# One VectorE filler calendar replaced by a fixed pattern, and gi laid out with the whole block as its last axis: a GRU and mixture-of-experts kernel

## What is computed

```python
def cell(h, x):                       # 512 times, B = 4, D = 512
    gi = x @ W_ih + b_ih              # r, z, n
    gh = h @ W_hh + b_hh
    r = sigmoid(i_r + h_r); z = sigmoid(i_z + h_z)
    n = tanh(i_n + r * h_n)
    return (1 - z) * n + z * h
...
x = x + moe_lora(scan(cell, cond_2048, x))          # layer 0
...
ix = (grid + 1) * 0.5 * (L - 1); x0 = floor(ix)     # layer 1
cond = w0 * x[x0] + w1 * x[x0 + 1]                  # along the features
x = x + experts_top2(cond)
```

## Time and profile before

| | |
|---|---|
| median of 3 runs | 2057.33 us (2053.76 to 2059.42) |
| the profiled execution | 2053.76 us, its span 2051.9 us |
| TensorE matmul busy | 1696.2 us, 83% |
| TensorE weight load busy | 1095.2 us, 53% |
| VectorE busy | 1410.8 us, 69% |
| ScalarE busy | 750.2 us, 37% |
| GpSimd busy | 285.6 us, 14% |
| mean granted TensorE clock | 0.966 |

### The profile page before, as it was taken

How to read it: one execution, slowest core, us unless ns; L and a number is a source line. 1 busy time by engine, 2 the same in 40 slices (tenths; PEclk the granted TensorE clock), 3 DMA queues, 4 the chain that set the end, 5 groups by cost and what they waited for, 6 DMA issues and landing times. The chain is left out here.

```text
span 2051.9 us, 90285 instructions
## 1 busy us (share of the span) xinstructions
PE 1696.2 (83%) x38301; PEld 1095.2 (53%) x38301; DVE 1410.8 (69%) x6376; ACT 750.2 (37%) x2706; POOL 285.6 (14%) x581
## 2 busy tenths in 40 slices
PE   6777767778679999968599999978699999776995
PEld 4565555555445556545456566545456555442442
DVE  6888888887757777767677777767677777641221
ACT  5544444442323343322233343323233333322332
POOL 0111111121121111120211011120211111201001
PEclk9999999999989999999899999989899999987997
DMA  8444343422055464422265555240545464228995
GB/s 311 174 145 157 129 157 141 157 95 85 22 204 193 172 248 176 144 64 64 85 213 185 210 214 178 82 116 3 186 183 193 172 213 152 69 60 304 348 356 164
DMA packets 113621, 334.86 MB, mean 163 GB/s; under 512 B 41920, under 2 KB 42168, under 8 KB 100800
## 3 DMA queue, kind: packets, MB, share of 16 engines
q1 hardware_dynamic: 108096, 312.31, 42.8%
q0 software_dynamic: 5120, 16.78, 2.5%
HBM read 263.74 MB, written 65.32 MB: 160 GB/s over the span
## 5 line engine op out<-in xcount | busy, mean ns | idle before, releaser
L480 PE MATMUL bank_g<-whh,hs_early 128*32 128x256 f16 x8192 | 324.6, 279 | 257.7 <-DVE hs_early L972 247.9
L1261 POOL COPY hxs<-hs 128x32 f16<-128x32 f16 x512 | 221.7, 433 | 1519.6 <-DVE hs L977 1519.6
L727 ACT ACTIVATE rz<-pre 128x32 f32<-128x32 f32 x512 | 118.9, 232 | 804.2 <-DVE pre L960 804.2
L480 PEld LDWEIGHTS bank_g<-whh,hs_early 128*32 128x32 f16 x8192 | 173.8, 97 | 435.0 <-DVE hs_early L972 424.0
L958 DVE STREAM_TRANSPOSE xt<-bank_g 128x256 f32<-128x256 f32 x512 | 229.7, 449 | 201.8 <-PE bank_g L486 196.4
L626 PE MATMUL bank<-wm,wih 128*128 128x512 f16 x1440 | 351.1, 384 | 2.8 <-issue 1.6
L493 PE MATMUL bank_g<-whh,hs 128*32 128x128 f16 x16384 | 331.4, 222 | 6.6 <-issue 6.1
L486 PE MATMUL bank_g<-whh,hs 128*32 128x256 f16 x8192 | 321.6, 278 | 1.4 <-issue 1.1
L493 PEld LDWEIGHTS bank_g<-whh,hs 128*32 128x32 f16 x16384 | 290.5, 99 | 14.0 <-issue 10.3
L727 ACT ACTIVATE seq_h<-na 128x16 f32<-128x16 f32 x512 | 111.6, 218 | 283.2 <-DVE na L966 283.2
L486 PEld LDWEIGHTS bank_g<-whh,hs 128*32 128x32 f16 x8192 | 191.1, 98 | 43.5 <-DVE hs L977 3.3
(11 more groups left out here) (139 smaller groups left out, 1863.4 us busy)
## 6 DMA issues: line engine op xcount, KB each, us to landing
wm<-moe_split SPq DMA_DIRECT2D x60, 1536.0 KB
wm<-moe_split SPq DMA_DIRECT2D x60, 1024.0 KB
wm<-moe_split SPq DMA_DIRECT2D x60, 512.0 KB
wm<-in_w_moe SPq DMA_DIRECT2D x16, 1536.0 KB, 10.9
moe_split<-wm SPq DMA_DIRECT2D x16, 1536.0 KB, 6.4
wih<-x_rows SPq DMA_DIRECT2D x60, 256.0 KB, 7.6
y_rows<-wih SPq DMA_DIRECT2D x60, 256.0 KB, 4.9
xr<-in_x SPq DMA_DIRECT2D x16, 512.0 KB, 7.0
```

Source lines behind the costliest of these rows:

```text
L480: mm(bank_g[0][32 * j:32 * j + 32, 0:2 * P], early_cols[:, 4 * B * k:4 * B * k + 32], whh[:, 1, k, at:at + 2 * P], start=(k == 0), stop=False)
L727: return nc.scalar.activation(dst, src, func, **kw)
L1261: Q.tensor_copy(hxs[:, par, :, :, :, col].rearrange("p s k b -> p s (k b)"), hs_new).then_inc(S["h_kept"], 1)
```

## The change

Two edits. First, the order of the fillers: GRID_AT is replaced by one pattern of steps for each sequence (GRID_STEPS, relative to step 32 b), whatever else stands in those steps; the layer-0 parts go to the VectorE steps 20 q + 10 and + 11, their ScalarE copy into step 20 q + 10 itself, and SyncE asks for the next grid row and the next layer-0 part at other steps. Second, gi is laid out as [128, 12, 4, 128]: the two halves lie side by side in each row of 128 time steps, so a half is 48 runs of 64 values. No arithmetic changes.

```diff
-def grid_steps():
-    at, s = {}, -1
-    for b in range(B):
-        s = max(s, 32 * b - 1)
-        for j in range(GRID_CHAIN):
-            s += 1 if j < 4 or j % 3 != 1 else 2
-            while s in X_LO or s in L0_LO or s == 97:
-                s += 1
-            at[s] = (b, j)
-    return at
+GRID_STEPS = (0, 2) + tuple(4 + 7 * k + o for k in range(K) for o in (0, 1, 4))
...
-        gi = sb("gi", [P, 2, G3, B, TB], F32)
+        gi = sb("gi", [P, G3, B, FT], F32)
...
+        def grid_at(s):
+            return s // 32, GRID_STEPS.index(s % 32) if s % 32 in GRID_STEPS else None
...
# sync: gi_half
-                sp.dma_start(gates_in[VISITS[v]]...[:, m], gi[:, at, m]
-                             ).then_inc(gi_stored[q], 16)
+                sp.dma_start(gates_in[VISITS[v]]...[:, m],
+                             gi[:, m, :, at:at + TB]).then_inc(gi_stored[q], 16)
...
-                if s % 32 == 5 and s // 32 + 1 < B:
+                if s % 32 == 3 and s // 32 + 1 < B:
...
-                if s - 3 in L0_AT[:3]:
-                    load_l0(L0_AT.index(s - 3) + 1)
+                if s % 20 == 15 and s // 20 < 3:
+                    load_l0(s // 20 + 1)
...
# sync: gi_load
-                sp.dma_start(gi[:, half].rearrange("p m b t -> p (m b t)"), gates_in[q]).then_inc(gi_in[half], 16)
+                sp.dma_start(gi[:, :, :, half * TB:(half + 1) * TB],
+                             gates_in[q].rearrange("p (m b t) -> p m b t", b=B, t=TB)).then_inc(gi_in[half], 16)
...
# scalar: gates_now
-                now = gi[:, col // TB, :, :, col % TB:col % TB + 1]
-                run(ext[:, 0:2 * K].unsqueeze(3), now[:, 0:2 * K], ACT.Copy)
+                at = bass.ds(col, 1) if not isinstance(col, int) else slice(col, col + 1)
+                run(ext[:, 0:2 * K].unsqueeze(3), gi[:, 0:2 * K, :, at], ACT.Copy)
...
# scalar: gi_out
-                run(gi[:, 1 if 0 < v < 5 else 0, m], bank...
+                at = TB if 0 < v < 5 else 0
+                run(gi[:, m, :, at:at + TB], bank...
...
# scalar: prelude
-                b, j = GRID_AT.get(s - 1, (0, 0))
-                if j and j % 3 == 0:
-                    grid_hi(b * K + (j - 2) // 3)
-                if s + 1 in L0_AT:
-                    l0_hi(L0_AT.index(s + 1))
+                if s:
+                    b, j = grid_at(s - 1)
+                    if j is not None and j >= 2 and j % 3 == 0:
+                        grid_hi(b * K + (j - 2) // 3)
+                if s % 20 == 10 and s // 20 < 4:
+                    l0_hi(s // 20)
...
# vector: prelude
-                if s in GRID_AT:
-                    grid_op(*GRID_AT[s])
-                if s in L0_LO:
-                    l0_lo(*divmod(L0_LO.index(s), 2))
+                b, j = grid_at(s)
+                if j is not None:
+                    grid_op(b, j)
+                if s % 20 in (10, 11) and s // 20 < 4:
+                    l0_lo(s // 20, s % 20 - 10)
```

More of the change, by code:

```diff
@@ L61 @@
 RW = P + E
[L66 to L69, removed]
-def grid_steps():
-    at, s = {}, -1
-    for b in range(B):
-        s = max(s, 32 * b - 1)
-        for j in range(GRID_CHAIN):
-            s += 1 if j < 4 or j % 3 != 1 else 2
-            while s in X_LO or s in L0_LO or s == 97:
-                s += 1
-            at[s] = (b, j)
-    return at
-GRID_AT = grid_steps()
+GRID_STEPS = (0, 2) + tuple(4 + 7 * k + o for k in range(K) for o in (0, 1, 4))
 def pieces(n, parts, slots):
@@ L283, in adaln_ffn_kernel @@
         GRU_CHAIN = 5
+        GRID_CHAIN = 2 + 3 * K
         def part_of(w, q):
@@ L339, in gi_half @@
                 sp.wait_ge(S["gi_done"], v * G3 + (q + 1) * (G3 // 2))
-                at = 1 if v < 5 else 0
+                at = TB if v < 5 else 0
                 m = slice(q * G3 // 2, (q + 1) * G3 // 2)
-                sp.dma_start(gates_in[VISITS[v]].rearrange("p (m b t) -> p m b t", b=B, t=TB)[:, m], gi[:, at, m]
-                             ).then_inc(gi_stored[q], 16)
+                sp.dma_start(gates_in[VISITS[v]].rearrange("p (m b t) -> p m b t", b=B, t=TB)[:, m],
+                             gi[:, m, :, at:at + TB]).then_inc(gi_stored[q], 16)
             load_x(1)
@@ L731, in gates_now @@
                 act.wait_ge(S["n_pre"], t)
-                now = gi[:, col // TB, :, :, col % TB:col % TB + 1]
-                run(ext[:, 0:2 * K].unsqueeze(3), now[:, 0:2 * K], ACT.Copy)
-                run(seq_n[:, :, 1:2].rearrange("p (k b) o -> p k b o", b=B), now[:, 2 * K:], ACT.Copy
+                at = bass.ds(col, 1) if not isinstance(col, int) else slice(col, col + 1)
+                run(ext[:, 0:2 * K].unsqueeze(3), gi[:, 0:2 * K, :, at], ACT.Copy)
+                run(seq_n[:, :, 1:2].rearrange("p (k b) o -> p k b o", b=B), gi[:, 2 * K:, :, at], ACT.Copy
                     ).then_inc(S["now_in"], 1)
@@ L757, in gi_out @@
                     act.wait_ge(gi_stored[m // (G3 // 2)], 16 * (v - 1 if v < 5 else v - 2))
-                run(gi[:, 1 if 0 < v < 5 else 0, m], bank[m % len(bank)][:, 0:N].rearrange("p (b t) -> p b t", b=B),
+                at = TB if 0 < v < 5 else 0
+                run(gi[:, m, :, at:at + TB], bank[m % len(bank)][:, 0:N].rearrange("p (b t) -> p b t", b=B),
                     ACT.Identity, bias=bi[:, m:m + 1]).then_inc(S["gi_done"], 1)
```

## The result

The changed kernel takes 2070.85 us (median of 5 runs, 2067.41 to 2077.68), the kernel before 2053.76 (5 runs): a ratio of 1.009, with a 95% interval of 1.0063 to 1.0115. It is 17 us slower. The forecast was 2063.0 us, some 6 us slower, with a range up to 2068; the time lies outside. They come from the single runs and are not exactly the quotient of the two medians, which is 1.0083 here.

What follows compares the result with a forecast made beforehand. VectorE with its fillers, or a 3.20 us floor, was taken to set the first 128 steps. Crowding +5.7 us net, layout 0: 2059.5 from the profiled 2053.76, 2063.0 us from the median 2057.33; range 2058 to 2068.

Steps and rivals of the forecast that it cites:

- The order of the fillers: First 128 steps of the recurrence: moving VectorE's filler work into other steps adds 5.7 us after corrections.
- step formula: First 128 steps: a step lasts the larger of 3.20 us and 2.89 plus its fillers, 0.48 or 0.63 each.
- the eleven crowded steps: First 128 steps: eleven with several fillers or a wait for ScalarE sum to 46.7 us; all 128 grow by 6.2.
- Rival 4: First 128 steps: a second filler runs in another engine's shadow and costs nothing; 2057 us, chance 0.05.
- a pause of TensorE would be covered in step 51: Step 51, three fillers: its 4.78 us cover a TensorE pause that left VectorE idle 0.42 us before; -0.5 us.
- The stride in ScalarE's reads: ScalarE's copies of gi, 512 instead of 256 bytes between elements: taken as 0, at most 2.8 us.
- The transfers: Ten stores and five loads of gi in 256-byte runs: a load grows 3.6 us, a store 1.8, all hidden.
- hidden, 0.7 left: First gi load: growth of at most 3.6 us fits the 4.3 us of room before L1107, which reads x.
- The pauses with releaser "issue": First 128 steps: TensorE pauses; pauses in all make 8.4 us of the measured 437.4.
- Rival 2: 256-byte runs slower than x's, so L1107 waits, or ScalarE's gi copies slower: 2066 to 2074 us, chance 0.1.
- Rival 1: Crowded steps idle TensorE and its clock falls one to three times, up to 1 us each: 2064 to 2066, chance 0.13.
- Rival 3: Crowded steps swallow the prelude's pauses, up to 7.9 us less: 2055.1 us; chance 0.05 with true gain, 0.07 without.

Runs made afterwards that it cites:

- the padded array: Kernel before, old tile layout, rows of gates_in in memory padded to twice their length so gi's stores and loads fall into 256-byte packets: 2046.41 us, ratio 1.0065.

## Why the prediction was wrong

**The order of the fillers: right.** The step formula held. Steps of two fillers took 3.85 to 3.96 us where it said 4.00, steps 10 and 30 4.34 and 4.32 (4.35), step 51 4.71 (4.78), and the eleven crowded steps together 45.8 (46.7). A filler behind a filler is a little shorter than behind L990, 0.68 and 0.47 us instead of 0.70 and 0.55, which explains the small surplus. The sum, +5.7 us, was measured as 0.32%, 6.5 us, and as 5.4 us between the medians of the preludes. Rival 4, no cost from crowding, falls with it. That a pause of TensorE would be covered in step 51 came true as well: it has no idle time before its next L945.

**The stride in ScalarE's reads: right.** 243 ns before and after.

**The transfers: this step failed.** The forecast priced the growth of a load at 3.6 us, and the median time to landing grew by 3.6, from 7.9 to 11.5. Part of that is luck: 1.57 MB at the 319 GB/s that it names are 4.9 us, while its 5.5 is the length of the window, so its own rates give +4.2; and the profiles with long runs on the other chips have 8.6 to 8.8 us to landing, which makes the growth 2.7 to 2.9. It then asked only who reads the data. It looked at L1107, for which there was room: L1095, its counterpart, is still released by TensorE. It passed over the loads in the middle of the expert slots with the sentence that there was more room elsewhere. The one that was late was not a reader of gi but the stream of TensorE's own instructions, q8, which the profile counts on the same 16 DMA engines. That belongs to the place where the forecast says "hidden, 0.7 left"; the term was 0 and measured 0.64%, 13 us.

The pauses with releaser "issue" were in the forecast, but as a fixed amount that crowded steps could cover or not. That they have a cause in the DMA and would grow with it wasn't asked, though the earlier trace rows show two of them. Rival 2 has the right part of the change and the wrong mechanism: it had L1107 wait for the load of x, or ScalarE's copies take longer, and neither happened. That the 2070.85 us lie in its 2066 to 2074 is luck.

What is shown: the loss comes with the loads as one transfer of 6,144 short runs, it is the same with the old tile layout, and it goes when each load is cut in four (1.0005). With two transfers of the same runs in the old layout there was none. In the changed kernel TensorE's next instruction packet doesn't start until all but some 15 of the load's 384 packets have; with the padded array it starts 7.1 us behind the issue, with about 1,900 short ones to come. Not separated are the count of the transfers, their size and the time over which SyncE issues them, which all change with a cut. Not settled either is what inside the DMA engines holds the packet back. The Trainium skill (DMA: Bandwidth & Descriptors, section "Queues, rings and completion order") has each engine alternate between queues packet by packet. By that, the instruction packet should wait for one packet of the load, which took 0.31 us here (4,096 bytes). The trace shows it 8.7 us behind the load's issue, and 4.1 with the load in parts, so the rule alone doesn't describe what happened. The Trainium skill's page "Runtime: NRT & Kernel Launch" (Instruction fetch mechanics) says that instructions are fetched over a DMA queue in 16 KB blocks, mostly hidden. The trace agrees with the first half (packets of 16 KB on q8), and not with the second here: 3.44 us in one place.

**Rival 1, the clock.** In the changed kernel's profile it fell once behind a crowded step. After step 70 (TensorE idle 2.13 us) L471 took 1.05 us instead of 0.61, and VectorE then waited 0.54 us:

```profile
293.64 0.64 PE L465 MATMUL bank_g<-whh,hs_early 128*32 128x256 f16 x16 [2.13 <-DVE hs_early L959]
294.09 1.05 PE L471 MATMUL bank_g<-whh,hs 128*32 128x256 f16 x16
...
295.18 0.45 DVE L945 STREAM_TRANSPOSE xt<-bank_g 128x256 f32<-128x256 f32 x1 [0.54 <-PE bank_g L471]
```

About half a microsecond, as small as it was put. It also fell behind the long stops, and a part of the 13 us is its price. Rival 3 (pauses swallowed) is refuted: it had the prelude shrink by about 2 us, and it grew by 8.0 in the one pair of profiles and by 5.4 between the medians.

## What to carry to other kernels

When a transfer becomes longer or falls into more pieces, its readers are not the only ones who can be late: look also at what else comes over the DMA engines, and first at the instruction stream of the engine that issues most. Pauses with releaser "issue" that stand at the same place in every profile mark the spots where it is already close, as step 202 did with its 0.46 us. Cut a large transfer of short runs into a few smaller ones, at times that differ if the deadline allows it; here that gave the whole loss back and cost nothing in time, though SyncE issues longer (6.01 us for the four parts at the start of block 1 with the new layout, 0.58 for the whole load).

A second piece of filler work in a gap that one piece has filled costs its full length; and a copy on one engine belongs a step ahead of the reader on another, not into the same step.

## What was not expected of the hardware

With a load of 1.5 MB in one transfer of 256-byte runs, the next 16 KB packet of TensorE's instructions starts 8.7 us behind the load's issue; with long runs it is 5.9, with the load in four parts 4.1. 6,144 runs in two transfers cost nothing measurable (0.9991), while in one they cost 0.65%. It makes no difference to that cost whether the runs travel as 384 packets of 4,096 bytes or as 6,144 of 256. A 1.5 MB copy in long packets behind the load costs nothing in the sum (0.9999), though a q8 packet is late beside it in block 2 as well. The stop of 3.44 us is followed by 3.4 us at the lower clock, so the step grew by 4.7.
